# Fewer directly multiplied column pairs, and the first chunks of the last stage loaded a unit early

## The reference

```python
x = x + layernorm(attention(layernorm(x)))          # 32 heads, 8 key/value groups, causal
g = einsum('bsh,ih->bsi', layernorm(x), Wg)         # Wg, Wu, Wd: (q - zero) * scale, groups of 64
u = einsum('bsh,ih->bsi', layernorm(x), Wu)         # inter = 2752
x = x + layernorm(einsum('bsi,hi->bsh', silu(g) * u, Wd))
```

## Time and profile before

| | us |
|---|---|
| median of three runs | 2773.65 |
| profiled execution, its own time | 2775.22 |
| its span, first to last instruction | 2773.4 |
| TensorE (PE) busy | 2639.6 (95%) |
| VectorE (DVE) busy | 1602.3 (58%) |
| GpSimd (POOL) busy | 1177.2 (42%) |
| ScalarE (ACT) busy | 952.8 (34%) |
| gate_and_up, first to last matmul | 1464.69 to 2281.5 |
| project_down, first matmul | 2301.74 |

### The profile page before, as it was taken

How to read it: one execution, slowest core, us unless ns; L and a number is a source line. 1 busy time by engine, 2 the same in 40 slices (tenths; PEclk the granted TensorE clock), 3 DMA queues, 4 the chain that set the end, 5 groups by cost and what they waited for, 6 DMA issues and landing times. The chain is left out here.

```text
span 2773.4 us, 42110 instructions
## 1 busy us (share of the span) xinstructions
PE 2639.6 (95%) x17064; PEld 1117.3 (40%) x17064; DVE 1602.3 (58%) x1986; ACT 952.8 (34%) x1674; POOL 1177.2 (42%) x654
## 2 busy tenths in 40 slices
PE   6999899999999999989978999999999998999998
PEld 3445533333333333324433444444444443444443
DVE  6332778778787787815668678777777760101001
ACT  3111266666666666661112222233223220000000
POOL 0000177777777777771223334555555540100001
PEclk8999999999999999999989999999999998999999
DMA  4223100011010110003223322333333328332220
GB/s 171 80 76 97 29 17 30 23 39 30 17 30 29 33 30 2 1 5 141 91 86 115 99 77 91 107 110 110 108 105 108 105 92 282 102 111 71 71 71 30
DMA packets 180047, 209.66 MB, mean 76 GB/s; under 512 B 17444, under 2 KB 138532, under 8 KB 179876
## 3 DMA queue, kind: packets, MB, share of 16 engines
q1 hardware_dynamic: 174148, 196.01, 21.7%
q10 hardware_dynamic: 5728, 11.27, 1.1%
HBM read 146.01 MB, written 61.08 MB: 75 GB/s over the span
## 5 line engine op out<-in xcount | busy, mean ns | idle before, releaser
L733 POOL TENSOR_TENSOR c_prob<-c_prob 128x1024 f32<-128x1024 f32 (+1 forms) x288 | 605.0, 2120 | 520.2 <-ACT c_prob L631 517.7
L647 DVE TENSOR_REDUCE c_maxes<-c_s 128x2 f32<-128x1024 f32 (+3 forms) x640 | 645.7, 1058 | 199.1 <-PE c_s L487 199.1
L631 ACT ACTIVATE c_prob<-c_s 128x512 f32<-128x512 f32 (+1 forms) x1152 | 598.0, 571 | 300.7 <-PE c_s L509 185.3
L509 PE MATMUL c_s<-c_q,c_k 97*128 97x512 f16 (+3 forms) x1280 | 367.3, 353 | 10.1 <-ACT c_prob L631 1.7
L1266 PE MATMUL e_ps<-x_hi,e_w_hi 128*128 128x512 f16 x832 | 316.1, 380 | 15.4 <-DVE e_w_lo L1339 15.4
L1267 PE MATMUL e_ps<-x_lo,e_w_hi 128*128 128x512 f16 x832 | 315.9, 380 | 0.0
L1268 PE MATMUL e_ps<-x_hi,e_w_lo 128*128 128x512 f16 x832 | 315.8, 380 | 0.0
L524 PE MATMUL c_ctx<-c_prob,v_sb 128*32 128x512 f32 (+3 forms) x2560 | 294.1, 540 | 0.2 <-ACT c_c L620 0.2
L1648 POOL TENSOR_TENSOR e_w<-e_w,e_scales 128x1024 f32<-128x1024 f32 (+2 forms) x67 | 161.5, 2410 | 263.5 <-DVE e_w L1323 263.5
L76 DVE BATCH_NORM_STATS2 f_norm_stats<-f_yp 128x6 f32<-128x512 f32 x16 | 11.2, 699 | 425.1 <-PE f_yp L1762 425.1
L509 PEld LDWEIGHTS c_s<-c_q,c_k 97*128 97x128 f16 x1280 | 111.3, 97 | 346.2 <-ACT c_prob L631 299.7
(11 more groups left out here) (167 smaller groups left out, 3589.6 us busy)
## 6 DMA issues: line engine op xcount, KB each, us to landing
h_hi<-e_hh SPq DMA_DIRECT2D x84, 128.0 KB, 1.9
h_lo<-e_hl SPq DMA_DIRECT2D x84, 128.0 KB, 1.8
b_x<-L_attn_x SPq DMA_DIRECT2D x16, 512.0 KB, 6.1
c_q<-qk_hi SPq DMA_DIRECT2D x64, 128.0 KB, 3.1
d_x<-L_attn_x SPq DMA_DIRECT2D x16, 512.0 KB, 5.2
x_dram<-d_x SPq DMA_DIRECT2D x16, 512.0 KB, 2.6
f_x<-x_dram SPq DMA_DIRECT2D x8, 1024.0 KB, 7.1
out<-f_z SPq DMA_DIRECT2D x8, 1024.0 KB, 5.0
```

Of the source, the lines that this page charges most:

```text
L509: last = nc.tensor.matmul(S2[:, h % 2, at:at + w], K[:, g % 2, k * P:(k + 1) * P], Q[:, g % 2, b, h, q:q + w], start=True, stop=not diag)
L631: nc.scalar.activation(prob(g, s, 0, w)[:, h, :], S2[:, h % 2, 0:w], ACT.Exp, scale=exp_scale).then_inc(exp_done, 1)
L647: last = nc.vector.tensor_reduce(MAXES[:, g % 2, t // TPB, heads, t % TPB, u], S1[:, heads, at:at + w], AX.X, ALU.max)
L733: return nc.gpsimd.tensor_tensor(one, one, two, ALU.add)
```

## The change

1. `PLAIN` goes from 5 to 3: direct pairs are gate 0, rest, up 0; gate 2 and up 2 join the seven-product pairs.
2. `made_beside` packs the eight T sums into five units instead of six: two, two, one, one, two. All four `make_t4` of p = 0 go into the last direct unit.
3. The second weight task of the first seven-product pair (`ahead`) is unpacked and scaled one unit earlier.
4. The rest pair's silu tiles go into S; the T tiles of p = 0 go into two new tensors `first_hi` and `first_lo`.
5. The two odd pieces of the down weights come first; their zeros and scales are loaded by one DMA for each run of 32 rows.
6. In the last unit, SyncE waits for P5 of the unit before it, then loads the first four chunks of down weights and of h (both halves of the first round, 3 MB in six DMAs) into `first_hi` and `first_lo`, ahead of the last stores. `project_down` waits only for these before its first matmul; SyncE, ScalarE and GpSimd wait for the stores inside it.

Cut to its core:

```diff
+FIRST = 4
-    PLAIN = 5
-    pairs = [("gate", 0), ("up", 0), ("rest", FULL), ("gate", 2), ("up", 2)]
-    pairs += [(kind, c) for c in range(4, FULL - 1, 2) for kind in ("gate", "up")] + [("both", FULL - 1)]
+    PLAIN = 3
+    pairs = [("gate", 0), ("rest", FULL), ("up", 0)]
+    pairs += [(kind, c) for c in range(2, FULL - 1, 2) for kind in ("gate", "up")] + [("both", FULL - 1)]
-    downs = [(m, half) for m in range(FULL // 2 + 2) for half in range(2)]
+    downs = [(m, half) for m in (FULL // 2, FULL // 2 + 1, *range(FULL // 2)) for half in range(2)]
+    AHEAD = (PLAIN - 1, 0)
+    ahead = beside[PLAIN - 1, 1][0]
-    made_beside = {(0, 0): [(0, 0)], (0, 1): [(0, 1)], (1, 0): [(0, 2)], (1, 1): [(0, 3)], (2, 0): [], (2, 1): [],
-                   (3, 0): [(1, 0), (1, 1)], (3, 1): [(1, 2), (1, 3)]}
+    made_beside = {(0, 0): [(0, 0), (0, 1)], (0, 1): [(0, 2), (0, 3)], (1, 0): [(1, 0)], (1, 1): [(1, 1)],
+                   (2, 0): [(1, 2), (1, 3)]}
...
+                            if downs[at][0] < FULL // 2:
+                                sp.dma_start(dst[:, slot, :], table[g:g + P // RUN, cols].unsqueeze(0)
+                                             .broadcast_to([RUN, P // RUN, BANK])).then_inc(raw_loaded[slot], 16)
+                            else:
+                                for r in range(n // RUN):
+                                    sp.dma_start(dst[first + r * RUN:first + (r + 1) * RUN, slot, :],
+                                                 table[g + r:g + r + 1, cols].broadcast_to([RUN, BANK])
+                                                 ).then_inc(raw_loaded[slot], 16)
...
+                if u == units[-1]:
+                    sp.wait_ge(product, product_no[units[-2] + ("P5",)])
...
+                    for i, (w, h) in enumerate(((wd_hi, h_hi), (wd_lo, h_lo))):
+                        sp.dma_start(first.weights(i), w[0:FIRST * P, :].rearrange("(c p) d -> p c d", p=P)
+                                     ).then_inc(first.loaded, 16)
+                        for of in range(2):
+                            sp.dma_start(first.rows(i, of), h[0:FIRST * P, of * 2 * P:(of + 1) * 2 * P]
+                                         .rearrange("(c p) t -> p c t", p=P)).then_inc(first.loaded, 16)
...
 @@ VectorE, gated @@
+                if u == AHEAD and name == hs(q)[-1]:
+                    unpack(ahead)
...
 @@ VectorE, plain, the last direct unit @@
+                    make_t4(0, 0)
+                    make_t4(0, 1)
+                    cut_t(0, 4, 0)
+                    cut_t(0, 4, 1)
                     gated(u, names[0])
+                    cut(q + 1, "S")
                     gated(u, names[1])
+                    make_t4(0, 2)
+                    make_t4(0, 3)
                     gated(u, names[2])
+                    cut_t(0, 4, 2)
+                    cut_t(0, 4, 3)
+                    cut(q + 1, "W2")
                     gated(u, names[3])
...
 @@ project_down @@
-    parts = [(0, 1), (1, 3), (3, 6), (6, 10), (10, APART), (APART, FULL)]
+    parts = [(FIRST, 8), (8, 12), (12, APART), (APART, FULL)]
...
+                if c == 0:
+                    pe.wait_ge(first.loaded, 16 * 6)
```

More of the change, by code:

```diff
@@ L1686, in _, with __init__, weights, rows @@
                 for name in hs(q):
+                    if u == AHEAD and name == hs(q)[-1]:
+                        scale(ahead)
                     trail(u, name)
-def project_down(nc, h_hi, h_lo, w_hi, w_lo, x1_dram, out, sem):
+    return ([(of[s], 16 * (len(h_no) // 2)) for of in (hi_stored, lo_stored) for s in range(2)]
+            + [(of, 16 * len(downs)) for of in (down_hi_stored, down_lo_stored)])
+class First:
+    def __init__(self, tiles, loaded):
+        self.tiles, self.loaded = tiles, loaded
+    def weights(self, i):
+        return self.tiles[i][:, 0:FIRST * 2 * BANK].rearrange("p (c d) -> p c d", c=FIRST)
+    def rows(self, i, of):
+        at = FIRST * 2 * BANK + of * FIRST * 2 * P
+        return self.tiles[i][:, at:at + FIRST * 2 * P].rearrange("p (c t) -> p c t", c=FIRST)
+def project_down(nc, h_hi, h_lo, w_hi, w_lo, first, stored_before, x1_dram, out, sem):
     D = w_hi.shape[1]
@@ L1718, in rows, with weights @@
             return bass.ds((2 * i + u) * BLOCK, BLOCK)
+        def weights(i, c):
+            return first.weights(i)[:, c] if c < FIRST else (wd_hi, wd_lo)[i][:, c - FIRST]
         @block.sync
@@ L1757, in _, with part_product @@
         def _(pe):
-            def part_product(u, s, c):
-                hh, hl = (h[:, u, c, s * P:(s + 1) * P] for h in (H_HI, H_LO))
-                for stat, w, a, z in ((hh, wd_hi, 1, 0), (hh, wd_lo, 0, 0), (hl, wd_hi, 0, 1)):
+            def part_product(u, s, c, opening):
+                if opening and c < FIRST:
+                    hh, hl = (first.rows(i, u)[:, c, s * P:(s + 1) * P] for i in range(2))
+                else:
+                    hh, hl = (h[:, u, c, s * P:(s + 1) * P] for h in (H_HI, H_LO))
+                wh, wl = (weights(i, c) for i in range(2))
+                for stat, w, a, z in ((hh, wh, 1, 0), (hh, wl, 0, 0), (hl, wh, 0, 1)):
                     for n in range(0, D, BANK):
-                        last = nc.tensor.matmul(YP[:, u, s, n:n + BANK], stat, w[:, c, n:n + BANK],
+                        last = nc.tensor.matmul(YP[:, u, s, n:n + BANK], stat, w[:, n:n + BANK],
                                                 start=(c == 0 and a == 1), stop=(c == CHUNKS - 1 and z == 1))
@@ L1766, in arrived @@
             def arrived(c):
-                for i, (first, end) in enumerate(parts):
-                    if c == first:
+                if c == 0:
+                    pe.wait_ge(first.loaded, 16 * 6)
+                for i, (start, end) in enumerate(parts):
+                    if c == start:
                         pe.wait_ge(w_loaded[i], 16 * (4 if end == FULL else 2))
```

123 lines of the change are left out of this document (68 added, 55 removed).

## The result

The changed kernel takes 2782.02 us (median of 8 runs, 2777.29 to 2783.07), the kernel before, run beside it, 2773.33: a ratio of 1.0029, 95% interval [1.0018, 1.0039]. It is slower by 8.7, where I had forecast 6.3 faster. The profiled execution took 2781.64 (span 2779.9; before 2775.22 and 2773.4).

What follows compares the result with a forecast made beforehand. It took gate_and_up to be bound by TensorE, with VectorE late at one transition and a DMA wait between the stages. +2.7 for the stage and -9.0 at the border gave -6.3: 2767.4 median, range 2753 to 2776.

Steps and rivals of the forecast that it cites:

- Term 1: TensorE's work in gate_and_up: four units go from 96 to 84 matmuls, saving 10.3 if VectorE delivers in time.
- the event: End of VectorE's W2 cut for the first seven-product pair: forecast at 1598.0; the stage gains only if before 1595.3.
- Term 2: When VectorE finishes that W2 cut in gate_and_up: at 1598.0, so the stage costs +2.7, matmul saving included.
- The gap at the up pair: TensorE waits some 10.6 for the up pair's W2, at its second product.
- the last direct unit: VectorE's four t4, T cuts, gated, S and W2: 15.4, plus a 0.6 wait for S, from 1579.5.
- 95.6: VectorE's full queue from the first T sum to the end of unit p = 0 of up, ending at 1579.5.
- the 2.5 that I had for subtractions: Stretching of VectorE by GpSimd's eight trail subtractions: between 0 and 10.4, taken as 2.5.
- one gap of 3 to 6, before P7: TensorE's gap in the first seven-product unit, before its first P7: 3 to 6.
- S is there in time: In the last direct unit, S is ready at 1586.0 against 1585.4, so VectorE waits only 0.6.
- The slower rival: Beside rest and up pairs, GpSimd's subtractions and sums hold VectorE in full: 13.1 later, +6.8, 2780.5; chance 0.10.
- Term 3: Border between the stages: with four chunks loaded early, TensorE starts at 2292.7 instead of 2301.74, -9.0.
- the tail: At the border, from the last down cut to TensorE's start: 7.2, as before.

Runs made afterwards that it cites:

- run 3: The change with GpSimd's four sums for the first seven-product pair waiting until the first two t4 are summed and cut; 2780.97 us, ratio 1.0029 to before.
- 13: The change with each t4 sum instruction of the last direct unit cut to 32 of 512 columns; 2771.89 us, ratio 0.9993 to before.
- Run 9: The change with five direct pairs in the old order, odd down pieces last and no early load; 2768.89 us, ratio 0.9987 to before.
- 5: The change with the odd, half-height down pieces last, as in the kernel before; 2778.77 us, ratio 1.0020 to before.
- 7: The change with five direct pairs in the old order and the odd down pieces last, early load kept; 2764.54 us, ratio 0.9969 to before.
- run 1: The change with the kernel before's five direct pairs and order of work, keeping early load and odd pieces first; 2764.75 us, ratio 0.9974 to before.

## Why the prediction was wrong

**Term 1 and the counting from the event held.** From W2's cut to the end of the stage it took 613.9 before and 685.7 after, 71.8 more; I had 72.3. So the stage's 11.0 is the event's own lateness.

**Term 2 held up to its last unit.** The gap at the up pair was 11.88 (I had 10.6), and the last direct unit began at 1580.21 (1579.5; 1.7 late, as the stage itself began 1.0 earlier than before). There is some luck in it: the first T sum began at 1481.09 (1483.9, so 1.8 early), and the queue behind it took 99.1 and not 95.6. The step that failed is the last direct unit, for which I had 15.4 + 0.6 + 2.5 = 18.5: it took 25.6 (1580.21 to 1605.78), 7.1 more. The first two t4 took 10.3 where I had 4.0, their cuts 2.3 for 1.2, the wait for S 2.15 for 0.6, the last two t4 4.9 for 4.0; the 2.5 that I had for subtractions covers a part. (The collision with the `ahead` scaling, 2.15, is among these, and I had counted it in the 95.6.) I also had one gap of 3 to 6, before P7; there were two, and the larger one, 11.71 before P6, is a wait for S, which I had called in time.

I wrote that "S is there in time" because from a scaling to S's cut it takes 7.9; here the scaling began at 1580.67 and not at 1577, held by a `trail`, and from it to S's low cut took 14.9 (1580.67 to 1595.60), since GpSimd's own rows were stretched (1.6 to 1.7 for the 1.26 that a sum took in run 3) and ScalarE's cut of S stood behind `lead`, `lead` behind `gated`, and `gated` behind the t4. I gave `trail` a price beside VectorE (2.5) and left the four sums without one: the clean row that I took it from had no VectorE work beside it, because there VectorE was waiting for exactly these sums. Runs 3 and 13 say how this splits: take the collision away and the wait takes its place; take nearly all t4 work away and S comes only 4.0 earlier, W2 7.5. It is a chain over engines that hold one another up, and my sum took each alone. Why S needs as long as it does in run 13 is not split further.

**The slower rival was near, in part by luck.** It had full hold-up by subtractions and sums, +6.8; measured is +8.7. But it placed the hold-up beside the rest and up pairs, where the queue took only 3.5 more than my sum, and not in the last direct unit; and two errors cancel: its event, 1611, was later than the 1606.8 (in before's time) that was measured, and its border was 6.0 too good. Run 3 also says that the hold-up is not a cause by itself: without the collision with the sums an equal wait stands there. By the Trainium skill (SBUF — State Buffer, "SBUF: two separate sides") a VectorE instruction with two SBUF inputs stands for the whole of a GpSimd instruction that reads SBUF and came first; the 32-column row of 2.23 beside a scaling that ended at 1581.50 agrees.

**Term 3 is the other failed step: -9.0 against -3.0.** That the down store would land in 4.3 and no longer in 10 is nearly right: 4.7 (2270.84 to 2275.54). Late were: the store's issue, 20.7 before TensorE's end and not 22.5 (1.8); from it to the last h store ahead of the loads, 14.8 and not 13.6 (1.2); from that store to the first load, 0.6; from the loads to the end of the last down cut, 14.9 and not 12.7, as six issues take 5.5 and the store behind them lands 7.0 after its issue (2.2); the tail, 7.6 and not the 7.4 that my times give (2285.3 to 2292.7, where I wrote 7.2) (0.2). Together they are the 6.0. Behind the sizes lies an error of account: I booked it as a gain that the odd pieces leave the last units, for their slow loads. Run 9, where they are still there, shows that one DMA for each run takes the wait from 13.70 to 6.52 without that. What their leaving costs is that full pieces take their place, and runs 5 and 7 price that at 6.5 and 10.1 of border. In the stage I counted the half-height pieces as shorter, rightly.

By the Trainium skill (DMA: Bandwidth & Descriptors, "Why a DMA increments its semaphore by 16 and not by 1") the old broadcasts could use only three or two engines. Run 9 agrees that they were what made the store slow, 13.70 to 6.52 of wait, though which engines were used no run here shows.

**The balance.** Each kernel's median against that of the kernel before in its own group: one DMA for each run -5.0 (before to 9), early load -4.1 (9 to 7), odd pieces first +0.4 (7 to 1, which is nothing), three direct pairs with what goes with them +17.3 (1 to after). The steps add up to the 8.7 because they are one chain; only the last is well clear of the intervals. In the stage alone the last step costs 18.2 (827.8 - 809.6) although 10.3 of matmuls are saved, so VectorE's side costs 28.5. The gaps grow from 3.1 to 26.8 (23.7). Matmuls started 0.43 apart instead of 0.2153 behind the gaps lose 6.4 in the change and 1.9 in run 1 (4.5). That makes 28.2.

What stays open: how much of the last direct unit an earlier unpacking of `ahead` would give back, which no run tried; and why the medians of runs 5 and 7 do not follow their stretches more closely than 3.
